# Weighing with 128-row by 64-column tiles: one PSUM sum per query half, in alternating banks

## The reference

```python
y   = relu(batchnorm(conv1_w @ x + conv1_b))          # 64 -> 16 channels, per pixel
wd  = conv2_w @ y + conv2_b                           # 9 taps per pixel
h   = sum over 9 taps of shifted x * wd               # dynamic 3x3 filter, one per pixel
h   = h.reshape(4, 4096, 64)                          # tokens of 64 features

n   = layernorm(h);  Q, K, V = n@Wq+bq, n@Wk+bk, n@Wv+bv
h   = h + softmax(Q @ K.T / 8) @ V                    # per image, 4096 x 4096 scores

n   = layernorm(h);  e = argmax(n @ router_w.T + router_b)     # one of 32 experts
h   = h + relu(relu(n @ W1[e] + b1[e]) @ W2[e] + b2[e])
```

## Time and profile before

| | us |
|---|---|
| median of 3 executions | 1120.71 (1116.73 to 1121.17) |
| the profiled execution, its own time | 1122.1 |
| its span, first to last instruction | 1120.2 |
| PE busy | 1091.2 (97%) |
| PE weight load busy | 538.7 (48%) |
| ACT busy | 584.5 (52%) |
| DVE busy | 528.5 (47%) |

### The profile page before, as it was taken

One profiled execution on the slowest core, in us unless ns is written; L12 is line 12 of the kernel. 1 busy time (PEld: TensorE's weight loads), 2 busy tenths in 40 slices (PEclk: granted clock), 3 DMA queues, 4 the chain that ended last, 5 costly groups with the idle time before them and its releaser, 6 DMA issues.

```text
span 1120.2 us, 28719 instructions
## 1 busy us (share of the span) xinstructions
PE 1091.2 (97%) x12476; PEld 538.7 (48%) x12476; DVE 528.5 (47%) x1039; ACT 584.5 (52%) x657; POOL 15.1 (1%) x48
## 2 busy tenths in 40 slices
PE   7799999999999999999999999999999999999997
PEld 3233333445444454555555455555555555554543
DVE  6688856428056372645537365463624141322305
ACT  2456666565646464554546455464545545454543
POOL 4010000000000000000000000000000000000000
PEclk6789999999999999999999999999999999999999
DMA  6636612122125222231412223140010101010000
GB/s 154 146 90 148 149 30 61 28 64 54 24 57 120 49 67 44 67 79 42 107 34 58 56 68 80 39 103 15 17 36 11 41 11 41 11 36 6 11 1 20
DMA packets 22385, 63.87 MB, mean 57 GB/s; under 512 B 3550, under 2 KB 7454, under 8 KB 21868
## 3 DMA queue, kind: packets, MB, share of 16 engines
q1 hardware_dynamic: 22172, 61.77, 23.3%
q10 hardware_dynamic: 80, 0.16, 0.0%
HBM read 53.31 MB, written 5.47 MB: 52 GB/s over the span
## 4 chain that ended last, share of the span: by engine, by line
PE 94%; DMA 2%; DVE 1%; ACT 1%; issue 1%; SPq 0%; DVEq 0%
PE z_ps L755 39%; PE scores L744 38%; PE both L596 5%; PE both L726 4%; PE both L587 2%; DMA filter_ring<-filters 1%; PE both L734 1%; DMA xin<-x_dram 1%; PE both L652 1%; PE both L642 1%; PE both L673 1%; PE both L692 1%; PE both L683 1%; PE scores L596 0%; PE both L718 0%
## 5 line engine op out<-in xcount | busy, mean ns | idle before, releaser
L979 ACT ACTIVATE probs<-scores 128x1024 f32<-128x1024 f32 x504 | 488.7, 1021 | 458.3 <-PE scores L744 458.3
L744 PE MATMUL scores<-g_t,keys_t 64*64 64x512 f32 x4096 | 513.9, 594 | 2.7 <-ACT g_t L958 1.2
L755 PE MATMUL z_ps<-probs,keys 64*64 64x512 f32 x4096 | 507.7, 591 | 0.0
L744 PEld LDWEIGHTS scores<-g_t,keys_t 64*64 64x64 f32 x4096 | 214.0, 134 | 235.3 <-issue 228.5
L755 PEld LDWEIGHTS z_ps<-probs,keys 64*64 64x64 f32 x4096 | 200.0, 133 | 187.1 <-issue 180.1
L1214 DVE SCALAR_TENSOR_TENSOR hidden<-both,chosen 128x1024 f32<-128x1024 f32 x44 | 53.9, 1225 | 200.6 <-PE both L596 186.4
L1154 DVE TENSOR_TENSOR hres<-hres,tap_product 128x504 f32<-128x504 f32 (+1 forms) x128 | 88.1, 688 | 11.2 <-issue 0.9
L1149 DVE SCALAR_TENSOR_TENSOR tap_product<-filter_ring,w,xin 128x504 f32<-128x504 f32 (+1 forms) x120 | 89.2, 743 | 7.8 <-DMA filter_ring<-filters 4.0
L596 PE MATMUL both<-y_t,w 64*64 64x512 f32 x448 | 60.9, 589 | 0.0
L726 PE MATMUL both<-hidden,w 64*64 64x512 f32 x448 | 56.8, 592 | 0.0
L1255 DVE COPY o_sb<-both 128x512 f32<-128x512 f32 x14 | 9.7, 691 | 85.2 <-PE both L726 85.2
(11 more groups left out here) (165 smaller groups left out, 558.2 us busy)
## 6 DMA issues: line engine op xcount, KB each, us to landing
filter_ring<-filters SPq DMA_DIRECT2D x90, 384.0 KB, 5.4
chosen<-choices SPq DMA_DIRECT2D x44, 256.0 KB
out_dram<-out_sb SPq DMA_DIRECT2D x32, 128.0 KB, 2.6
xin<-x_dram SPq DMA_DIRECT2D x6, 528.0 KB, 10.8
g_t<-g_t SPq DMA_DIRECT2D x24, 128.0 KB, 6.3
hidden<-once_dram SPq DMA_DIRECT2D x1, 930.0 KB, 15.5
choices<-onehot_t SPq DMA_DIRECT2D x22, 32.0 KB, 1.6
hidden<-once_dram SPq DMA_DIRECT2D x1, 576.0 KB, 7.2
```

Of the source, the lines that this page charges most:

```text
L744: last = T.matmul(scores[rows_of(h), c, r * 512:(r + 1) * 512], keys_t[rows_of(r), i // NQ % 2, k * 128 + 64 * h:k * 128 + 64 * h + 64], g ...
L755: last = T.matmul(z_ps[rows_of(c), h, :], keys[rows_of(h), i // NQ % 2, 2 * k + r, :], probs[rows_of(h), (2 * g + c) % RING, r * 512:(r + ...
L979: A.activation(probs[:, unit % RING, :], scores[:, c, :], ACT.Exp, scale=first_scale[:, 0:1] if n == 0 and g <= ASKED else SCALE).then_inc ...
```

## The change

`into_z` uses tiles of 128 rows and 64 columns: the loop over h is gone, a matmul has all 128 keys of a key tile as its rows, and each block has one sum instead of two. It issues 4 matmuls per step in place of 8. The one sum of a segment needs one bank; `bank_of` chooses it so that neighbouring segments use different banks. Because of that a segment's first weighing waits for the copy of the segment before the last one, not of the last one. `z_part` and `keep_part`'s copies are half as large, and `whole_z` has one instruction where it had two or three. Nothing else in the program is changed: `score` and all fills keep their tiles.

```diff
+def bank_of(n, g):
+    return g // HALF % 2 if n < 2 else n % 2
...
-        z_part = sb("z_part", [128, 3, 2, 512])
+        z_part = sb("z_part", [128, 3, 512])
...
                 for r in range(2):
-                    for h in range(2):
-                        for c in range(2):
-                            last = T.matmul(z_ps[rows_of(c), h, :], keys[rows_of(h), i // NQ % 2, 2 * k + r, :],
-                                            probs[rows_of(h), (2 * g + c) % RING, r * 512:(r + 1) * 512],
-                                            start=(begins(n, g) and r == 0), stop=(ends(n, g) and r == 1))
+                    for c in range(2):
+                        last = T.matmul(z_ps[rows_of(c), bank_of(n, g), :], keys[:, i // NQ % 2, 2 * k + r, :],
+                                        probs[:, (2 * g + c) % RING, r * 512:(r + 1) * 512],
+                                        start=(begins(n, g) and r == 0), stop=(ends(n, g) and r == 1))
...
                 if begins(n, g) and (n or g):
-                    if n < 2:
-                        pe.wait_ge(z_kept, 2 * n + g // HALF)
-                    else:
-                        pe.wait_ge(z_copied, n)
+                    if n > 1:
+                        pe.wait_ge(z_copied, n - 1)
+                    elif n:
+                        pe.wait_ge(z_kept, 2 * n + g // HALF - 1)
...
-                    A.copy(z_part[:, 2 * n + g // HALF - 1, :, :], z_ps[:, :, :]).then_inc(z_kept, 1)
+                    A.copy(z_part[:, 2 * n + g // HALF - 1, :], z_ps[:, 1 - bank_of(n, g), :]).then_inc(z_kept, 1)
...
                 if i == 0:
                     dve.wait_ge(z_kept, 3)
-                    V.tensor_tensor(z_part[:, 0, :, :], z_part[:, 0, :, :], z_part[:, 2, :, :], ALU.add)
-                    settle()
-                    V.tensor_tensor(z_sb[:, :], z_part[:, 0, 0, :], z_part[:, 0, 1, :], ALU.add).then_inc(z_copied, 1)
+                    V.tensor_tensor(z_sb[:, :], z_part[:, 0, :], z_part[:, 2, :], ALU.add).then_inc(z_copied, 1)
                 elif i == 1:
-                    V.tensor_tensor(z_part[:, 0, 0, :], z_part[:, 1, 0, :], z_part[:, 1, 1, :], ALU.add)
-                    settle()
                     dve.wait_ge(pv_done, 2 * PAIRS)
-                    V.tensor_tensor(z_sb[:, :], z_part[:, 0, 0, :], z_ps[:, 0, :], ALU.add)
-                    settle()
-                    V.tensor_tensor(z_sb[:, :], z_sb[:, :], z_ps[:, 1, :], ALU.add).then_inc(z_copied, 1)
+                    V.tensor_tensor(z_sb[:, :], z_part[:, 1, :], z_ps[:, bank_of(1, HALF), :], ALU.add).then_inc(z_copied, 1)
                 else:
                     dve.wait_ge(pv_done, (i + 1) * PAIRS)
-                    V.tensor_copy(z_sb[:, :], z_ps[:, 0, :])
-                    settle()
-                    V.tensor_tensor(z_sb[:, :], z_sb[:, :], z_ps[:, 1, :], ALU.add).then_inc(z_copied, 1)
+                    V.tensor_copy(z_sb[:, :], z_ps[:, bank_of(i, 0), :]).then_inc(z_copied, 1)
```

## The result

The changed kernel takes 1195.61 us (median of 4 runs, 1191.56 to 1196.09) against 1120.08 for the kernel before (4 runs): 1.066 times, 95% interval 1.0644 to 1.0677, 75.5 us slower. The forecast was 1192.

What follows compares the result with a forecast made beforehand. PE's array time was taken to bound the kernel (busy 97%, steady quads all stream). Profiled 1122.1 us + 70.6 for 504 shape changes - 0.8 at the end = 1192 us; range 1145 to 1228.

Steps and rivals of the forecast that it cites:

- Streaming: Weighing on PE: half as many records, two side by side, four turns of 0.43 us, 1.72 us as before: 0.
- A change of shape: PE at each edge of a 128*64 weighing among 64*64 work: 0.14 us a change, bounds 0.105 and 0.21.
- the idle stream: Array left empty at a change of tile shape: 0.10 us at full clock, 0.13 at half clock.
- the uncovered load: Weight load that starts with its matmul, not ahead of it, after a shape change: 0.03 us at full clock.
- stagger: Offset between the starts of tiles sharing the array, at each shape change: 0.01 us.
- The count: 255 runs of weighing make 510 shape changes, 504 of which cost: 504 x 0.14 = +70.6 us.
- the six changes ahead of it: Changes of the three weighings before the first `keys` wait: 0.8 us, going into PE's 6.64 us wait for DVE.
- Sums and waits: Segment starts and removed DVE adds: 0; at the end `z_sb` is ready sooner without its add: -0.8 us.
- The free change: Rival: no drain between 64*64 and 128*64 on PE, only the last add gained, 1121 us; 11%.
- Only one direction: Rival: only the way into or out of 128 rows costs, 252 x 0.14 = 35, 1157 us; 5%.
- Records that cost time by themselves: Rival: 2048 fewer matmul records on PE save 0.014 us each, 29 us, so 1093 us without a drain; 4%.
- Halves that take turns: Rival: with 128 rows the two column halves don't run side by side, +440 us, 1562 us; 4%.

Runs made afterwards that it cites:

- scores_128: The changed kernel with the score at 128*64 too, 4 matmuls for 8, half of the scores not computed: 1174.09 us against the changed kernel's 1195.61.
- one_bank_128: The changed kernel with all its sums in bank 0 and the waits of the kernel before: 1194.90 us against the changed kernel's 1195.61.

## Why the prediction was right

*What bounds the kernel.* Right: no wait that the change relieves was on the path but one, and only the array's time per step counted.

*Streaming: 0.* Right. Two column halves do run side by side with 128 rows, for which there had been no row: 1.72 us in scores_128.

*A change of shape: 0.14 us.* Right in kind, a little low: 0.150 by the spans, 0.146 to 0.157 in the other kernels that reorder or replace the same matmuls. Its parts were the idle stream, taken as 0.10 (between 0.065, if all of it went by the array's clock, and 0.13), measured 0.09; the uncovered load, taken as 0.03, measured 0.05; and stagger, taken as 0.01, measured 0.01 to 0.02. The load is the mis-sized term. I had read it from a record of 0.62 against 0.59, where a small matmul stood before and part of the load was still covered: it started at 600.28 for a matmul at 600.31. That the sum came within 0.01 us a change is partly luck, since the idle stream was taken 0.01 too high and the load 0.02 too low, and 0.10 was a choice between bounds of 0.065 and 0.13. At half clock the idle stream was 0.13, so doubling the clock took away 0.04 of it, a third and not a half.

The Trainium skill, "TensorEngine Tiling (Array Packing)", Key Properties, says that a change of tiling mode drains TensorE; the runs agree with it for rows (32 and 128 against 64) and for columns (128 against 64). By my estimate from the Trainium skill, "TensorE: Matmul & The Clock Gate", Single matmul latency, the warm drain would have been about 0.12 and the whole 1202 us; 0.09 was measured, and the measurement decides.

*The count: 504 that cost.* The difference from the turn of `keys` to the end, 75.0 us, is as good as the whole difference of the medians, 75.5. That agrees with the six changes ahead of it going into DVE's wait, but doesn't show it: they would be 0.9 us, less than the 4.5 us between the fastest and the slowest run. Kernels with 282, 504 and 924 changes that count, each against its control, and the one with some 137 taken away lie within 0.146 to 0.157 us a change, so the count carries the time. The trace of the changed kernel has the 510: 255 from 64*64 to 128*64 and 255 back.

*Sums and waits: 0, and -0.8 at the end.* Right: one_bank_128 is level, and the wait of `pz` went from 1.6 to 0.9 us.

*The rivals.* The free change fell with the first timeline. Only one direction: both cost the same, 0.07 us of overlap left on either side of a weighing. Records that cost time by themselves: 2048 fewer brought nothing, and 8 records of 128*64 take the 1.72 us of 16 records of 64*64. Halves that take turns: no.

## What to carry to other kernels

In this kernel, where TensorE streams f32 matmuls of 512 columns without a gap, what counted was not how many matmuls there are but where the tile shape changes. Write down the sequence of shapes in PE's order and count the changes; here each cost 0.15 us at full clock. A shape that looks more natural for one stage costs a change at each edge unless its neighbours have it too, and that weighs the more the shorter the stage is; here each group of 1.72 us was paid for with a change of 0.15. To price such a change from a trace that has few of them, compare the modelled end of a group with the start of the next: 0.07 us of overlap where the shape changes against 0.17 and more where it doesn't (606.69 and 606.52 in scores_128).

## What the runs showed of the hardware that I had not expected

A matmul of one column on a single quarter of the array, in an unchanged shape, cost 0.11 us of PE's time in the middle of a full stream (29.2 us for 256), nearly as much as a change of shape over that control (0.122). And a 1-column matmul at 64*128 added 0.055 us a change over the one at 128*64 (0.177 against 0.122): the loads of twice the weight columns take 0.10 us more (0.29 against 0.19), and once the shape has changed all of it shows in the distance to the next matmul (0.31 against 0.21).
